# Attention and mixture of experts on one core: activation rows turned between products of up, normalisation shared by two engines, logits one step earlier

## What is computed

```python
xn = _layernorm(x, axis=-1)
x = x + _L0_attn_ref(xn, ...) + _L0_ffn_ref(xn, ...)
# attention: 8 heads of 32, blocks of 12 queries, 24 keys each (12 before them, 12 of their own)
matrix_ac = jnp.einsum('bnchd,bnkhd->bhnck', q_blocked, k_ctx)
matrix_bd = _rel_shift(jnp.einsum('bnchd,phd->bhncp', q_blocked, rel_k))
logits = jnp.tanh((matrix_ac + matrix_bd) / SOFTCAP) * SOFTCAP
attn = jax.nn.softmax(logits, axis=-1)
# experts: rms norm, softmax over 8 router logits, top 2, weights renormalised
hidden = jax.nn.silu(gate) * up                            # 704 values
out_e = jnp.einsum('bsh,dh->bsd', hidden, down_weight[e])
moe_out = moe_out + combine[..., e, None] * out_e
return x + alpha * moe_out                                 # ffn: x is xn
```

## Time and profile before

| | us |
|---|---|
| median of three runs | 811.63 |
| lowest and highest | 808.91, 815.01 |
| profiled execution | 807.16 |
| its span, first to last instruction | 805.4 |
| busy in the span: TensorE, DVE, ACT, POOL | 766.4, 459.9, 345.8, 406.3 |

### The profile page before, as it was taken

How to read it: one execution, slowest core, us unless ns; L and a number is a source line. 1 busy time by engine, 2 the same in 40 slices (tenths; PEclk the granted TensorE clock), 3 DMA queues, 4 the chain that set the end, 5 groups by cost and what they waited for, 6 DMA issues and landing times.

```text
span 805.4 us, 20445 instructions
## 1 busy us (share of the span) xinstructions
PE 766.4 (95%) x6909; PEld 749.8 (93%) x6909; DVE 459.9 (57%) x1057; ACT 345.8 (43%) x621; POOL 406.3 (50%) x309
## 2 busy tenths in 40 slices
PE   6599999999999999899999999999999999999993
PEld 5599999899999999899999999999999999999992
DVE  5475537788888775535555555555555555555551
ACT  5467546566655555523333333333333333333330
POOL 3667956777785666703333333334444434444322
PEclk9899969999999999799999999999999999999997
DMA  7643786889995454102246265264265363222211
GB/s 253 205 145 119 239 268 220 275 285 318 308 306 175 136 111 120 52 25 41 40 123 178 41 176 124 42 178 122 49 170 121 94 179 68 39 42 44 39 27 20
DMA packets 65327, 111.07 MB, mean 138 GB/s; under 512 B 15617, under 2 KB 47277, under 8 KB 65229
## 3 DMA queue, kind: packets, MB, share of 16 engines
q0 software_dynamic: 19760, 45.11, 22.9%
q1 hardware_dynamic: 33997, 44.13, 18.7%
q10 hardware_dynamic: 11472, 20.47, 7.9%
HBM read 66.60 MB, written 42.75 MB: 136 GB/s over the span
## 4 chain that ended last, share of the span: by engine, by line
PE 86%; DMA 4%; POOL 3%; ACT 2%; issue 2%; DVE 2%; SPq 1%; ACTq 0%; POOLq 0%; DVEq 0%
PE psum L1271 78%; PE psum L1384 4%; DMA arena<-bd_d 1%; POOL xn_all L623 1%; DMA bd_d<-arena 1%; PE psum L1342 1%; DMA out<-spare,sca_i 1%; PE psum L1460 1%; PE psum L1315 1%; POOL w_ring L597 1%; PE psum L1290 1%; DMA x_all<-in_x 1%; PE psum L1469 0%; ACT psum L814 0%; ACT arena L795 0%
## 5 line engine op out<-in xcount | busy, mean ns | idle before, releaser
L1271 PE MATMUL psum<-w_ring,xT 128*128 x1608 | 284.6, 328 | 1.9 <-issue 1.3
L1271 PEld LDWEIGHTS psum<-w_ring,xT 128*128 128x128 f32 x1608 | 258.1, 190 | 2.3 <-issue 2.3
L674 POOL DMA_INDIRECT out<-spare,sca_i x67 | 106.3, 1586 | 252.9 <-DVE spare L1258 238.4
L1271 PE MATMUL psum<-w_ring,hT 128*128 x1139 | 151.8, 287 | 2.2 <-DVE spare L1258 1.5
L1271 PEld LDWEIGHTS psum<-w_ring,hT 128*128 128x128 f32 x1139 | 140.2, 190 | 2.5 <-issue 2.5
L776 ACT ACTIVATE xT<-psum,nwp 128x128 fp32r<-128x128 f32 x134 | 41.9, 364 | 192.2 <-PE psum L1342 156.6
L1135 DVE SCALAR_TENSOR_TENSOR xT<-psum,nwp,xT 128x128 fp32r<-128x128 f32 x134 | 40.8, 346 | 119.5 <-ACT xT L776 110.1
L1124 DVE SCALAR_TENSOR_TENSOR spare<-psum,xg,spare 128x704 f32<-128x704 f32 x67 | 63.7, 950 | 76.1 <-PE psum L1271 76.1
L650 POOL TENSOR_TENSOR arena<-arena,const 120x540 f32<-120x540 f32 x38 | 59.2, 1558 | 77.5 <-ACT arena L818 77.5
L885 ACT ACTIVATE hT<-psum 128x768 fp32r<-128x768 f32 x67 | 54.4, 812 | 99.9 <-PE psum L1384 98.4
L1271 PE MATMUL psum<-arena 32*120 32x108 f32 (+1 forms) x1216 | 89.8, 268 | 0.0
(11 more groups left out here) (174 smaller groups left out, 1001.9 us busy)
## 6 DMA issues: line engine op xcount, KB each, us to landing
w_split<-w_ring POOLq DMA_DIRECT2D x20, 1088.0 KB, 7.0
w_ring<-w_split SPq DMA_DIRECT2D x40, 544.0 KB
raw<-in_w_raw ACTq DMA_DIRECT2D x32, 544.0 KB, 5.7
arena<-in_x SPq DMA_DIRECT2D x37, 108.0 KB
out<-arena SPq DMA_DIRECT2D x37, 108.0 KB
arena<-xn_d SPq DMA_DIRECT2D x31, 120.0 KB
bd_d<-arena SPq DMA_DIRECT2D x38, 84.4 KB
xn_d<-xn_all POOLq DMA_DIRECT2D x3, 1024.0 KB, 7.8
```

The costliest lines, as they stand in the source:

```text
L674: pool.indirect_dma_start(out=out, out_offset=bass.IndirectOffsetOnAxis(ap=sca_i[:, b:b + 1], axis=0), in_=y[:, b % 2, :], in_offset=None, ...
L1271: return pe.matmul(out_ap, lhs, rhs, start=first, stop=last)
```

## The change

Seven edits, in the order of the diff.

1. `S_L` is 3: the router's tiles are in steps 3 to 10, and the routing and the tables are one step earlier.
2. ScalarE normalises tiles 18, 19, 22, 23, 26, 27, 30 and 31 at the end of steps 6 to 9, and POOL the others of the second half. The stores of tiles 16 to 23 and 24 to 31 are issued by ScalarE, in steps 7 and 9, not by POOL.
3. On SP's queue the two transfers of window 3 come before the first write of biases, not after it.
4. ScalarE issues the loads of x tiles 16 to 23 and 24 to 31 in steps 2 and 3, not 1 and 2.
5. In steps 2 and 3 the copy of the band and the evacuation of the transposed biases come later in ScalarE's and DVE's order: behind the queries, and behind the biases.
6. `turn_biases` in these steps is behind keys and biases on TensorE.
7. In blocks 2 to 63 the six transpositions of the activation rows of block `b - 1` stand singly behind every second product of up of block `b`.

```diff
-        S_L = 4
+        S_L = 3
...
+        ON_ACT = [t for t in range(TT) if t < X0 or t >= 2 * XCH and t % 4 >= 2]
+        ON_POOL = [t for t in range(TT) if t not in ON_ACT]
...
+        XN_STORED = {3: 7, 4: 9}
...
             for s in range(NG + NSTEP):
+                if s == 0:
+                    load_window(NWIN)
                 if s < NG:
                     flat_out(s)
-                if NWIN <= s + 3 < NG:
+                if NWIN < s + 3 < NG:
                     load_window(s + 3)
...
                 for t in late_tiles(s):
-                    layernorm(t)
-                    for i in range(1, len(PARTS)):
+                    if t in ON_POOL:
+                        layernorm(t)
+                    for i in range(1, 3):
                         if t == PARTS[i][1] - 1:
                             store_xn(i)
...
@@ scalar: behind the evacuation of the queries
+                if s in LATE:
+                    repeat(s - 2)
                 if lt:
                     normed_evac(lt[2])
                     normed_evac(lt[3])
-                if 1 <= s < 3:
-                    load_part(s + 2)
+                if s == S_D[3] + 1:
+                    act.wait_ge(s_nb, 4)
+                for t in late_tiles(s):
+                    if t in ON_ACT:
+                        normalise(t, t + 1)
+                for i in XN_STORED:
+                    if s == XN_STORED[i]:
+                        store_xn(i)
+                if 2 <= s < 4:
+                    load_part(s + 1)
...
@@ tensor: gate_up
+                    between = 1 < b < NB_MIN and j >= 2
+                    if between and j == 2:
+                        hidden_there(b - 1)
                     for k in range(KD):
-                        for px, pw in PASSES:
+                        for i, (px, pw) in enumerate(PASSES):
...
+                            n = (j - 2) * KD * len(PASSES) + k * len(PASSES) + i
+                            if between and n % 2:
+                                turn_chunk(b - 1, n // 2)
...
@@ tensor: the steps
                 if s < NG:
                     biases(s)
+                if s in LATE:
+                    turn_biases(s - 2)
...
                 stage(pe, blocks, b, gate_up)
-                stage(pe, blocks, b - 1, turn_h)
+                if not 1 < b < NB_MIN:
+                    stage(pe, blocks, b - 1, turn_h)
                 stage(pe, blocks, b - 2, down)
```

More of the change, by code:

```diff
@@ L391, in program @@
         CHUNKS = [(0, X0), (X0, XCH), (XCH, 2 * XCH), (2 * XCH, TT)]
-        XND = X0
+        ON_ACT = [t for t in range(TT) if t < X0 or t >= 2 * XCH and t % 4 >= 2]
+        ON_POOL = [t for t in range(TT) if t not in ON_ACT]
         S_D = {1: 0, 2: 2, 3: 5}
         def normalised(eng, t):
-            if t < XND:
-                eng.wait_ge(s_xn, t + 1)
-            else:
-                eng.wait_ge(s_xnd, t - XND + 1)
+            if t in ON_ACT:
+                eng.wait_ge(s_xn, ON_ACT.index(t) + 1)
+            else:
+                eng.wait_ge(s_xnd, ON_POOL.index(t) + 1)
+        XN_STORED = {3: 7, 4: 9}
         def logit_tiles(s):
@@ L711, in store_xn @@
                 first, last = PARTS[i]
-                normalised(act, last - 1)
+                for t in range(last - 4, last):
+                    normalised(act, t)
                 act.dma_start(tile_rows(xn_d, i), xn_all[:, first:last, :]).then_inc(s_xnst[i], 16)
@@ L747, in round_piece @@
                 if e == 2:
-                    act.wait_ge(s_xnd, TT - XND)
+                    for t in range(TT - 4, TT):
+                        normalised(act, t)
                 under = piece_under(n)
@@ L842, in _ @@
                     deviation(1)
-                if s in LATE:
-                    repeat(s - 2)
                 if lt:
@@ L1203, in _ @@
                     spread_of(1)
-                if s in LATE:
-                    turned_biases(s - 2)
                 if s < NG:
@@ L1216, in _ @@
                                     psum[0:GQ, 5, D:D + H * NPOS].rearrange("p (h n) -> p n h", h=H)).then_inc(s_bde, 1)
+                if s in LATE:
+                    turned_biases(s - 2)
                 if 0 <= s - 4 < NG:
@@ L1346, in _, with hidden_there, turn_chunk @@
             slots = [None] * NB
+            def hidden_there(b):
+                pe.wait_ge(s_h, b + 1)
+                if b:
+                    pe.wait_ge(s_hta, b)
+                    pe.wait_ge(s_htb, b)
+            def turn_chunk(b, c):
+                ins = pe.transpose(moved(psum[:, 4 + c // 3, (c % 3) * P:(c % 3 + 1) * P]),
+                                   hb_m[:, b % 2, c * P:(c + 1) * P], ident_m)
+                if c == HCH - 1:
+                    ins.then_inc(s_ht, 1)
             def gate_up(b):
@@ L1378, in turn_h @@
             def turn_h(b):
-                pe.wait_ge(s_h, b + 1)
-                if b:
-                    pe.wait_ge(s_hta, b)
-                    pe.wait_ge(s_htb, b)
+                hidden_there(b)
                 for c in range(HCH):
-                    ins = pe.transpose(moved(psum[:, 4 + c // 3, (c % 3) * P:(c % 3 + 1) * P]),
-                                       hb_m[:, b % 2, c * P:(c + 1) * P], ident_m)
-                ins.then_inc(s_ht, 1)
+                    turn_chunk(b, c)
             def down(b):
@@ L1570, in _ @@
                     queries(s)
-                if s in LATE:
-                    turn_biases(s - 2)
                 if lt:
```

## The result

| | before | changed |
|---|---|---|
| median, 20 runs each | 821.69 | 829.44 |
| lowest and highest | 807.11, 837.69 | 823.23, 877.65 |
| profiled execution | 807.16 | 827.09 |
| its span | 805.4 | 825.3 |
| mean granted clock | 0.971 | 0.963 |

The changed kernel is slower: the ratio is 1.02, interval 1.0163 to 1.0236. The ratio compares only executions within 1.5% of each kernel's fastest, which is why it is further from one than the ratio of the medians. The forecast was 810.3 against 811.63, no change that can be measured.

A forecast was written before the change was run, and what follows sets the result against it. TensorE, busy nearly everywhere, was taken as the bound, with a hole near 100 us. Terms 7.7 - 8.3 + 1.0 - 2.25 + 0.5 = -1.35 us gave 810.3 us against the median 811.63, range 796 to 819.

The forecast's parts named there:

- Turns, +7.7: Expert stage, 62 blocks: lone transpositions can't hide the next product's 0.109 us load, +0.124 us a block, +7.7 us.
- Rivals 1 and 2: Expert stage: loads run ahead of more than one matmul, 794.5 us (12%); the transposition's place costs nothing, 802.6 us (10%).
- Hole at 100 us, -8.3: Attention: POOL relieved, the 2.2 us TensorE hole and 6.1 us of work at lower clock go, -8.3 us.
- -2.25: Logits from step 3: step 11 loses its logits, -2.25 us; waits in step 3 partly absorb those it takes on.
- rival 3: Steps 7 to 11: ScalarE delays or crowded DMA queues make another hole and the clock falls anyway, 816.4 us; 15%.
- ScalarE's delay, +1.0: Steps 6 to 9: added normalisations and stores ahead of tanh overrun 0.6 us of cover, +1.0 us.
- rival 4: Steps 7 to 10 wait for ScalarE, needing normalisations to pay for table loads or more delay: 822 us; 8%.
- First biases, +0.5: Steps 2 and 3: biases turned late and SP reordered, step 2 2.5 us shorter, step 3 3 us longer, +0.5 us.
- -9.05: The attention stage's gain, about 9 us, as subtracted from the median 811.63 us in the rivals' sums.
- a wait near 2 us as the point that decides: Attention: no clock fall followed 0.96 us idle at 62.96, one followed 1.91 at 102.07; a hole near 2 us decides.

The follow-up runs named there:

- tiles alone: Kernel before with only ScalarE normalising and storing half of the second half's tiles: 815.1 against 821.85, ratio 0.9898.
- the changed kernel, filled: Changed kernel with 11 unused products of 256 columns where TensorE waits in steps 2 and 3: 817.15 against 818.92 of before, ratio 1.0049.
- router alone: Kernel before with only the router's tiles moved to steps 3 to 10 (`S_L` is 3): 857.48 against 821.85, 6 runs.
- the later router: Kernel before with the router in steps 5 to 12 (`S_L` is 5): 825.11 against 821.62, ratio 1.0116.
- router and tiles: Kernel before with router from step 3, tiles split with ScalarE, and 17 unused products in the waits: 810.27 against 815.52, ratio 0.9992.
- all but the turns filled: Changed kernel without the single transpositions, with 11 unused products in the waits of steps 2 and 3: 814.39 against 821.62, ratio 0.9906.
- all but the turns: Changed kernel without the single transpositions in the expert blocks: 858.26 against 821.85 of before, 6 runs.
- step 2 filled, step 3 not: Changed kernel with only the seven unused products of step 2: 855.67 against 820.3 of before, ratio 1.0279, 4 runs.
- router alone, filled: Kernel before with router tiles from step 3 and 12 unused products in the waits of steps 2 and 3: 814.69 against 820.3, ratio 0.9946.
- pairs: Kernel before with a block's six transpositions in three pairs between products of up: a block takes 6.685 us against 6.615; one execution, 832.7.

## Why the prediction was wrong

**Turns, +7.7: right, a little small.** The mechanism held as written: the load behind a lone transposition takes 0.11, the place decides, no load starts two ahead. The block came out at 6.759, not 6.73. The term used 0.109 for the load; the 0.113 of the narrow products gives 6 x 0.113 - 0.53 = 0.148 a block, 9.2 us, and 8.9 were measured. Rivals 1 and 2 fell. The Trainium skill ("TensorE: Matmul & The Clock Gate", on loading the stationary operand) gives an estimate of 107 ns for any load of 128 columns; the 0.11 behind a lone transposition is near it, and the 0.084 inside the group, on which the loss rests, is not.

**Hole at 100 us, -8.3: right.** In the changed kernel the two gaps are 8.42 and 7.41 where they were 14.55 and 12.28, -11.0 with the router's step; the terms -8.3 and -2.25 make -10.55. The tiles alone give 8.4 and 9.2, which is -9.2. Some 1.2 of either is ScalarE catching up with what the next paragraph tells. The clock did not fall between 90 and 120 us, so rival 3 as it was placed did not come.

**ScalarE's delay, +1.0: right.** Between the exponentials of groups 3 and 7 the changed kernel takes 40.3 where before took 38.2, and the kernel with the tiles alone 40.4. The steps grew by 1.0, 0.7, -0.2 and 0.7. The first of these is two normalisations ahead of tanh, 0.99 us from the start of the first to the instruction after. Timeline of ACT, changed kernel:

```profile
82.30 1.08 ACT L714 ACTIVATE xn_all<-x_all,small 128x256 f32<-128x256 f32 x2
83.29 0.21 ACT L881 ACTIVATE small<-small 128x32 f32<-128x32 f32 x1
83.52 1.28 ACT L823 ACT_TABLE_LOAD   x1
```

But that is ScalarE falling behind, and TensorE lost less. Its transpositions of the biases in steps 5 and 9, before and in the changed kernel (that of step 9 before is in the earlier trace rows):

```profile
52.62 0.28 PE L1460 MATMUL psum<-turns,arena_m 108*128 108x108 f32 x2
...
67.36 0.40 PE L1491 MATMUL psum<-turns,arena_m 108*128 108x108 f32 x2
...
106.45 0.28 PE L1491 MATMUL psum<-turns,arena_m 108*128 108x108 f32 x2
```

The four steps took TensorE 90.78 - 52.62 = 38.16 before and 106.45 - 67.36 = 39.09 now, 0.9 more.

The table load there is no new one: it stood at 67.69 in the kernel before as well. The normalisations brought no table load of their own, so the condition of rival 4 did not come.

**First biases, +0.5: right only where the clock is kept.** Alone the three edits measured 825.99 against 818.92, ratio 1.0159, and beside the tiles the new order made 1.011 of 0.9898. In the changed kernel, filled, the first exponential comes 0.7 earlier and that of group 3 1.7 later than before, with the router's tiles of step 3 in it. The bias write took 4.88 and started at 19.30, 1.4 later, as worked out from SP's queue.

**The step that failed is the price of steps 2 and 3**: the router's term, -2.25 with "they fill part of it", and the first biases' +0.5. Both counted where time goes and nothing for TensorE's clock. What the runs showed in its place: the early router alone made 857.48 of 821.85, the new order cost 1.6% alone and 2.1% (some 17 us) beside the tiles, and with the waits of these steps filled the same edits without the turns came out at 0.9906 [0.9847, 0.9966], where the forecast's -9.05 of 811.63 is 0.9889. So the sum of the attention terms held where the clock was kept, and what it left out is the clock. In step 3 the first router tile fills nothing: it waits 1.36 us itself, behind ScalarE's table load, and step 3 gets 16 products of 8 columns and eight transpositions, which began a step further from the waits before. In the profiled execution the clock stayed at 0.50 for 30.7 us, in that with edit 1 alone for 99; filled, group 3 comes +1.7 late and not +14.9. How the loss of the changed kernel divides between the two terms stays open: each brings it alone, and together they don't add up.

**What the text had read.** It weighed a fall of the clock only for steps 7 to 11 and took a wait near 2 us as the point that decides, from one pair of rows. Steps 2 and 3 had waits of 3.57, 1.12 and 1.38 us in the kernel before, with a low stretch (25.4 to 32.3 us) about the first, and were not looked at. The one profile also was of a quick execution: it doesn't show the 27.3 us of low clock that the same code had there in two others.

**A wait outside the forecast**, the +4.6 between groups 9 and 11. Rival 3 names crowded DMA queues, but only up to step 11. Chain of waits of the changed kernel, 128 to 143 us:

```profile
128.38 6.27 DMA bd_d<-arena
...
135.99 6.00 DMA arena<-bd_d
...
142.61 0.43 PE psum L1491 x2
```

The biases' way to memory and back took 12.3 us of transfers, where a step now takes 7.4, and TensorE stood 2.67 us for them at 142.61; the clock was low until 146.1. The same two legs took 4.88 and 2.80 in step 0. Faster steps ask for the band sooner, while the weights crowd the DMA engines, which were busy to 0.90 then. Window of the changed kernel:

```profile
128.40:142.00 13.60, 11.17 (x146) 10.38 (x142) 10.59 (x25) 6.51 (x11) 9.93 (x8) 1.00 0.90 297
```

That the crowd is the cause was argued, not tried.

**Three things stay open**: why a fall comes, and how long it lasts, in one execution and not in another of the same code; why the later router gained nothing; and why router and tiles don't add up.

## What to carry to other kernels

Transpositions of 128 columns belong together, not between wide products: alone, each leaves the next product's load uncovered (0.11 us here, 62 x 0.144 = 8.9 us in all). Before narrow work is moved next to a kernel's waits, read the granted clock there and price the stretch that follows at half speed; TensorE's busy share does not show it. Where waits of a microsecond or two can't be removed, a dozen unused wide products in them are worth trying: with them the changed kernel ran in 817.15 instead of 829.44, though one execution in 12 was still at 855.51. Where executions fall in groups, profile more than one before a sum is built on it. The best here, the half of the tiles on ScalarE with or without such products, and all but the turns filled, are about 1% or less under the kernel before.

## What the runs showed of the hardware

- At 0.50 a stream with hardly a gap did not bring the clock back for 99 us (99.00 of 99.00 busy, router alone) and 140 us (137.51 busy, all but the turns); in another execution of the latter's steps (the changed kernel) it was back after 30.7. The Trainium skill ("TensorE: Matmul & The Clock Gate", "What's actually happening") says that activity releases the throttle; what the trace calls busy is not enough for it here. The same part of that page puts the price of the slow start below 1% of a typical span; that is the ramp at the start alone, and here falls in midstream cost 36 us of 822 in the router alone.
- With 15 wide products more in five steps the stretch behind step 3 lasted 37.5 us in the profiled execution, and the median was 34 us lower.
- Waits of 0.63, 0.93 and 1.37 us were followed by a fall that lasted 130 us (step 2 filled, step 3 not), and in another kernel (router alone, filled) waits of 0.71, 0.97 and 1.37 by none. No size of wait that decides could be read.
- A transposition behind another costs 0.084 us, and alone between wide products 0.11; pairs lie between (0.070 a block for three places against 0.144 for six). No load in these rows starts more than one matmul ahead.
